# First stage of a two-layer attention and expert kernel: projection placed directly behind the scores, tables cleared from SP's queue, first expert's rows loaded at the stage's end

## The chip, the cores and the metric

The kernel runs as one launch on one core of a Trainium2 chip. The metric is the device time of that core in microseconds (us). The time of the kernel before is 1819.05 us, the median of three runs (1818.01 to 1819.5).

## The reference, cut to what matters

Eight sequences of 100 rows of 512 values pass through two layers. Each layer is an attention over a context and then a mixture of 8 experts, of which each row uses the best two:

```python
x = x + xattn0(layernorm(x), ctx)     # 16 heads of 32, causal: of 722 context rows only the first 100 count
x = x + ffn0(layernorm(x), ...)       # norm again, logits over 8 experts, top 2, gelu(x W1 + b1) W2 + b2, weighted; adds x again
x = x + xattn1(layernorm(x), ctx)     # 16 heads of 64, own rows and 722 context rows as keys
x = x + ffn1(layernorm(x), ...)       # top 2 of 8, silu(gate) * up, down, norm
```

Inside `xattn0`: `q = x q_w + q_b`, `k = ctx k_w + k_b`, `v = ctx v_w + v_b`, `softmax(q k^T / sqrt(32)) v`, then `o_w`, `o_b`. All is float32.

## The kernel before, in words

`build` (L2073) runs seven stages one after the other, and `end_stage` (L100) closes each: GpSimd clears the semaphores, and a barrier of all engines follows. In `front`, the stage that is changed, a barrier also ends its block of five engine programs (L318). The stages are `front` (attention of layer 0, and the routing of each row to its experts), `experts` layer 0, `combine` 0, `project`, `attend`, `experts` layer 1, `combine` 1.

`front` works through the eight sequences, one cycle `b` for each. Every engine has its own program, written out by hand, and runs it strictly in order; semaphores join them. Queries and keys are projected for two sequences at a time (a pair `g` has blocks "q" and "k"), in halves of 16 products into banks 6 and 7. `block_at(b)` (L313) says which block cycle b makes: "k" of pair b//2+1 in even cycles, "q" in odd ones, none in cycles 6 and 7.

The programs in cycle b, before the change:

- TensorE (L575 to L607): `scores(b)` into banks 0 to 3; `values(b)` into bank 4, once `scaled(b-1)` on VectorE has read it (`yn`); `route_logits(b-2)` into bank 7; `output(b-1)` into bank 5; `route_rank(b-2)` into bank 7; the projection `project_pair` (L452); `turn_x(b+3)` into bank 5, after `add_output(b-1)` has read it (`os_`); `turn_probabilities(b)` in four groups q = 0 to 3 into banks 6 and 7, of which q = 1 waits until `route_slot(b-2)` has read bank 7 (`rkc`); `route_turn(b-1)`; `attended(b)`. In cycle 0 a product of the value bias with the output weights (L583) stands behind `values`, and writes `ob`, on which `turn_x(3)` waits (`obs`).
- VectorE (L731 to L756): `scaled`, `highest`, `route_best`, in cycle 0 `vb_wide`, the low part of `o_w` and `ob` (L738 to L742), `add_output`, `route_slot`, `normalise_rows(b+3)`, `projected` (reads banks 6 and 7, adds the bias), `context_low`, `input_stats(b+5)`, `route_rows(b-1)`. After cycle 7 follow `route_best`, `route_slot` and `r.passes`, which lays out the table of expert passes.
- ScalarE (L832 to L845): `attended_high`, `exponents`, `values`, in cycle 0 `weights_high` of `o_w`, `context_high` in even cycles, `turned_x`, `turned`, `route_turned`.
- GpSimd (L412 to L433): `route_root(b-1)`, `root_in(b+5)`, `add_bias(b+1)`; in cycles 0 to 3 twelve transfers each (eleven in the last) that write zeros of 512 KB over the tables `slot_rows` and `slot_outs` in device memory; from cycle 5 on the scatters that put normalised rows into their slots, two for each sequence, after `zeroed`.
- SP (L333 to L368) issues loads: inputs, weights, the context of each pair, and ahead for the next stage three chunks of expert weights.

`experts` layer 0 makes passes of 256 rows. Before its loop SP loads b1, gamma and beta (L917 to L919) and the first rows `xs` (L930, L943); TensorE turns the rows (L984), VectorE (L1052) and ScalarE (L1115) apply gamma and beta once all three constants are in (`c_in` 48, L1037 and L1099), the rows are split into high and low parts (L1123, L1058), and the first product (L1005) starts.

Of the kernel before, what the change touches and what calls it, by code (L numbers as in the profile page):

```python
# [37 lines left out]
CAP = 256  # L38
# [196 lines left out]
def front(k, ahead0):  # L235
# [4 lines left out]
    ZERO_CYCLES = 4  # L240
    with ExitStack() as c:
# [65 lines left out]
        e_hi = k.sem("e0_hi_ahead")  # L307
# [10 lines left out]
        with nc.Block() as block:  # L318
            @block.sync
            def _(sp):  # L320
                def x(b):
                    sp.dma_start(k.x[:, b, :], a["x"][b]).then_inc(x_in[b], 16)
# [29 lines left out]
                for b in range(5, B):  # L352
                    x(b)
                for g in range(2, PAIRS):
                    sp.wait_ge(pjs, first_half(g - 2, "k") + 2)
                    sp.wait_ge(cld, g - 1)
                    context(g)
                for q in range(ahead0.LOADED):
                    if q == 0:
                        sp.wait_ge(wld, 1)  # L360
                    elif q == 1:
                        sp.wait_ge(wld, 2)
                        sp.wait_ge(obm, 1)
                    else:
                        sp.wait_ge(pj, first_half(PAIRS - 1, "k") + 2)
                    sp.dma_start(ahead0.raw[q][:], a[ahead0.names[q][0]][ahead0.names[q][1]]).then_inc(raw_in[q], 16)
                for q in range(ahead0.LOADED):
                    sp.wait_ge(raw_in[q], 16)  # L368

            @block.gpsimd  # L370
            def _(pool):
# [37 lines left out]
                pool.wait_ge(zmade, 1)  # L409
                pool.wait_ge(obs, 1)  # L410
                per = -(-len(ZERO_ROWS) // ZERO_CYCLES)
                for b in range(B):  # L412
                    if b >= 1:
                        route_root(b - 1)
                    if b + 5 < B:
                        root_in(b + 5)
                    if b == 0:
                        add_bias(0)
                    if b + 1 < B:
                        add_bias(b + 1)  # L420
                    if b < ZERO_CYCLES:
                        for dst, n in ZERO_ROWS[per * b:per * (b + 1)]:
                            pool.dma_start(dst[CAP * n:CAP * (n + 1)].rearrange("(p s) d -> p (s d)", p=128),
                                           zero[:]).then_inc(zeroed, 16)
                    if b == 5:
                        pool.wait_ge(zeroed, 16 * len(ZERO_ROWS))
                    if b >= 5:
                        scatter(2 * (b - 5))
                        scatter(2 * (b - 5) + 1)
# [6 lines left out]
            def _(pe):  # L436
# [138 lines left out]
                for b in range(B):  # L575
                    scores(b)
                    values(b)
# [8 lines left out]
                    if b >= 2:  # L586
                        route_logits(b - 2)
# [4 lines left out]
                    if block_at(b):  # L592
                        if b >= 1:
                            pe.wait_ge(ts, 4 * b)
                        else:
                            pe.wait_ge(pjs, 4)
                        project_pair(*block_at(b), ranked=b - 1)
# [18 lines left out]
            def _(dve):  # L616
# [114 lines left out]
                for b in range(B):  # L731
                    if b >= 1:
                        scaled(b - 1)
                    highest(b)
                    if b >= 2:
                        route_best(b - 2)
                    if b == 0:
                        dve.wait_ge(c_in, 32)  # L738
                        nc.vector.tensor_copy(vb_wide[:], bc(vb[:], T)).then_inc(vbw, 1)
                        weights_low(2, wo, "o")  # L740
                        dve.wait_ge(obm, 1)
                        nc.vector.tensor_tensor(ob[:], ob[:], ps[0:T, 5, :], ALU.add).then_inc(obs, 1)  # L742
                    if b >= 1:
                        add_output(b - 1)
                    if b >= 2:
                        route_slot(b - 2)
                    if b + 3 < B:
                        normalise_rows(b + 3)
                    if block_at(b):
                        projected(*block_at(b))  # L750
                    if b % 2 == 0 and b // 2 + 1 < PAIRS:
                        context_low(b // 2 + 1)
                    if b + 5 < B:
                        input_stats(b + 5)
                    if b >= 1:
                        route_rows(b - 1)  # L756
# [12 lines left out]
            def _(act):  # L769
# [62 lines left out]
                for b in range(B):  # L832
                    if b >= 1:
                        attended_high(b - 1)
                    exponents(b)
# [3 lines left out]
                    if b % 2 == 0 and b // 2 + 1 < PAIRS:  # L839
                        context_high(b // 2 + 1)  # L840
# [11 lines left out]
def experts(k, layer, first, s1=None):  # L852
# [18 lines left out]
    with ExitStack() as c:  # L871
# [6 lines left out]
        xs = k.sb(c, L + "xs", [128, 2, D])  # L878
# [34 lines left out]
        with nc.Block() as block:  # L913
            @block.sync
            def _(sp):
                if not gated:
                    sp.dma_start(b1[:], a["b1"]).then_inc(c_in, 16)  # L917
                    sp.dma_start(gam[:], a["gam0"]).then_inc(c_in, 16)
                    sp.dma_start(bet[:], a["bet0"]).then_inc(c_in, 16)  # L919
# [23 lines left out]
                rows(0)  # L943
# [622 lines left out]
class FirstWeights:  # L1566
# [4 lines left out]
    def __init__(self, k, ctx, layer, parts=None):  # L1571
# [5 lines left out]
        self.hi, self.lo = parts  # L1577

# [561 lines left out]
```

## Time and profile before

| | us |
|---|---|
| median of three runs | 1819.05 |
| the profiled execution's own time | 1819.06 |
| its span, first to last instruction | 1817.3 |
| TensorE matmul busy | 1644.4 (90%) |
| VectorE busy | 1080.6 (59%) |
| ScalarE busy | 764.2 (42%) |
| GpSimd busy | 156.2 (9%) |
| mean granted TensorE clock | 0.946 of full speed |

The profile is of one execution. PE is TensorE's matmuls, PEld its weight loads, DVE VectorE, ACT ScalarE, POOL GpSimd, SP the engine that only issues transfers; a q behind a name means that engine's queue. In a timeline a row has the start, the duration, the engine, the line, the operation, output <- input by the program's names, the shapes and the count; in square brackets stands how long the engine was idle before, and who released it. The granted clock is 1.00 at 2.4 GHz and 0.50 at 1.2 GHz. The stage `front` takes the first 228 us of the span, `experts` layer 0 follows.

### The profile page before, as it was taken

How to read it: one execution, taken by the hardware profiler on the slowest of the kernel's cores; microseconds unless marked ns; L12 is line 12 of the kernel's file. 1: busy time of each engine (PE TensorE's matmuls, PEld its weight loads, DVE VectorE, ACT ScalarE, POOL GpSimd, SP SyncE). 2: the span in 40 equal slices, each digit the busy share in tenths (PEclk: the TensorE clock that was granted, in tenths of full speed). 3: DMA queues.
4: the chain of work that ended last, by engine and by line, in shares of the span. 5: the costliest groups of instructions: out<-in, count | busy, mean ns of one | idle time of the engine just before them, and what ended most of it. 6: DMA issues, size and time to landing. Idle time of an engine off the chain costs nothing. (4 is left out here: it accounts for less than half of the span.)

```text
span 1817.3 us, 31629 instructions
## 1 busy us (share of the span) xinstructions
PE 1644.4 (90%) x11976; PEld 1392.7 (77%) x11976; DVE 1080.6 (59%) x1968; ACT 764.2 (42%) x1348; POOL 156.2 (9%) x208
## 2 busy tenths in 40 slices
PE   6888479999999779979999999999999759999984
PEld 5776369999999469768787877878787559999981
DVE  3666656666777652236565655656565557667666
ACT  2333245555555332235354443535353324454440
POOL 1442200000000300100000000000000000000004
PEclk9998689999999889989999999999999769999996
DMA  5871155555555434240111101110202045556534
GB/s 161 333 291 37 37 210 208 208 208 206 204 204 202 135 123 167 82 133 18 47 44 31 52 23 48 27 57 17 60 24 85 10 150 208 209 184 229 208 127 117
DMA packets 86571, 232.81 MB, mean 128 GB/s; under 512 B 33326, under 2 KB 39854, under 8 KB 71374
## 3 DMA queue, kind: packets, MB, share of 16 engines
q1 hardware_dynamic: 68446, 175.52, 28.4%
q0 software_dynamic: 18032, 55.99, 8.7%
q8 instruction: 66, 1.08, 0.2%
q14 instruction: 27, 0.22, 0.0%
HBM read 180.41 MB, written 51.05 MB: 127 GB/s over the span
## 5 line engine op out<-in xcount | busy, mean ns | idle before, releaser
L1727 PE MATMUL banks<-a_ch,a_wm 128*128 128x362 f32 (+1 forms) x1024 | 285.8, 340 | 10.4 <-DVE a_cl L1888 10.4
L1042 DVE TENSOR_TENSOR e_lo<-e_raw,e_hi 128x2048 fp32r<-128x2048 f32 x98 | 224.4, 2290 | 94.8 <-ACT e_hi L1106 94.8
L1005 PE MATMUL banks<-e_xh,e_hi 128*128 128x256 f32 x768 | 217.5, 283 | 4.2 <-DVE e_xl L1058 4.2
L1005 PE MATMUL banks<-e_xh,e_lo 128*128 128x256 f32 x768 | 217.9, 284 | 0.0
L1005 PE MATMUL banks<-e_xl,e_hi 128*128 128x256 f32 x768 | 217.9, 284 | 0.0
L1106 ACT CAST e_hi<-e_raw 128x2048 fp32r<-128x2048 f32 x98 | 186.7, 1905 | 29.4 <-PE banks L1022 29.4
L1727 PEld LDWEIGHTS banks<-a_ch,a_wm 128*128 128x128 f32 x1024 | 186.1, 190 | 12.2 <-DVE a_cl L1888 11.8
L1901 DVE TENSOR_REDUCE a_nmax<-banks 100x1 f32<-100x822 f32 x128 | 123.6, 1007 | 76.1 <-PE banks L1761 75.3
L1727 PE MATMUL banks<-a_cl,a_wm 128*128 128x362 f32 (+1 forms) x512 | 168.8, 330 | 0.0
L1005 PEld LDWEIGHTS banks<-e_xh,e_hi 128*128 128x128 f32 x768 | 147.3, 192 | 10.4 <-issue 4.6
L1022 PE MATMUL banks<-e_hi,e_hh 128*128 128x512 f32 x384 | 152.6, 397 | 0.0
L1005 PEld LDWEIGHTS banks<-e_xl,e_hi 128*128 128x128 f32 x768 | 147.3, 192 | 5.3
L1022 PE MATMUL banks<-e_lo,e_hh 128*128 128x512 f32 x384 | 150.9, 393 | 0.0
L1022 PE MATMUL banks<-e_hi,e_hl 128*128 128x512 f32 x384 | 149.6, 390 | 0.0
L1005 PEld LDWEIGHTS banks<-e_xh,e_lo 128*128 128x128 f32 x768 | 147.3, 192 | 0.0
L2011 ACT ACTIVATE a_P<-banks,a_nmax 100x822 f32<-100x822 f32 x128 | 120.7, 955 | 11.1 <-DVE a_nmax L1901 10.9
L1772 PEld LDWEIGHTS banks<-ident,a_P 100*128 100x128 f32 (+2 forms) x896 | 82.2, 137 | 34.1 <-issue 31.8
L1140 ACT ACTIVATE e_hf<-banks,e_b 128x256 f32<-128x256 f32 x128 | 59.7, 473 | 112.8 <-PE banks L1005 112.7
L1761 PE MATMUL banks<-a_kT,a_q 64*100 64x512 f32 (+1 forms) x512 | 105.3, 530 | 0.0
L1772 PE MATMUL banks<-ident,a_P 100*128 100x100 f32 (+2 forms) x896 | 101.8, 254 | 3.0 <-ACT a_PT L2019 3.0
L1005 PE MATMUL banks<-e_xh,a_wm 128*128 128x256 f32 x512 | 96.2, 287 | 8.8 <-DVE e_hf L1071 5.5
L1727 PEld LDWEIGHTS banks<-a_cl,a_wm 128*128 128x128 f32 x512 | 98.0, 192 | 0.0
(280 smaller groups left out, 3019.9 us busy)
## 6 DMA issues: line engine op xcount, KB each, us to landing
e_raw<-wout SPq DMA_DIRECT2D x50, 1024.0 KB, 7.8
e_raw<-w SPq DMA_DIRECT2D x34, 1024.0 KB, 6.1
e_raw<-wgate SPq DMA_DIRECT2D x17, 1024.0 KB, 5.0
e_raw<-wup SPq DMA_DIRECT2D x17, 1024.0 KB, 5.1
slot_rows<-a_zero POOLq DMA_DIRECT2D x33, 512.0 KB, 9.2
a_craw<-ctxT SPq DMA_DIRECT2D x32, 361.0 KB
e_xs<-slot_rows SPq DMA_DIRECT2D x18, 512.0 KB
slot_outs<-e_y POOLq DMA_DIRECT2D x16, 512.0 KB, 3.2
```

What stands on the lines that cost most here:

```text
L1005: mm = nc.tensor.matmul(ps[:, bank, 0:CAP], w[:, cc, cut], x[:, cc, :], start=t == 0, stop=t == len(terms) - 1)
L1022: mm = nc.tensor.matmul(ps[:, 4 + s, :], h[q % 4][:, cut], w[:, q % 4, :], start=q == 0 and t == 0, stop=q == NB - 1 and t == 2)
L1042: nc.vector.tensor_tensor(lo[g % 2][i], raw[q % RAW][:], hi[g % 2][i].bitcast(F32), ALU.subtract)\
L1106: nc.scalar.copy(hi[g % 2][i], raw[q % RAW][:]).then_inc(hi_done, 1)
L1140: nc.scalar.activation(hf[kb % 4][:], ps[:, kb % 4, 0:CAP], ACT.Gelu, bias=b1[:, bass.ds(e * NB + kb, 1)]).then_inc(f_done, 1)
L1727: mm = nc.tensor.matmul(ps[:, 6 + half, 0:wide], w[:, cc, cut], x[:, cc, start:start + wide], start=cc == 0 and t == 0, stop=cc == DC - 1 ...
L1761: mm = nc.tensor.matmul(ps[0:T, 2 * two + f, 0:wide], q[s][r, :], kT[s][r, first:first + wide], start=True, stop=True)
L1772: mm = nc.tensor.transpose(ps[0:size, 4 + n // 5, T * (n % 5):T * (n % 5) + T], P[(2 * m + two) % 4][:, first:first + size], k.ident[0:T, ...
L1901: nc.vector.tensor_reduce(nmax[:, h:h + 1], two_banks(2 * two)[0:T, 0:KEYS], AX, ALU.max, negate=True)\
L2011: nc.scalar.activation(P[h % 4][:], two_banks(2 * two)[0:T, 0:KEYS], ACT.Exp, bias=nmax[:, h:h + 1], accum_out=sums[:, h:h + 1]).then_inc( ...
```

## The change

Three edits of `front`, with their counterpart in `experts`. First, on TensorE the projection of cycle b stands directly behind `scores(b)`, before `values(b)`; `route_logits`, which writes a bank that the projection has filled, waits until VectorE has read it. On VectorE `projected`, `context_low`, `normalise_rows` and `input_stats` move up, behind `highest`; in cycle 0 `normalise_rows(3)` stays behind `ob`. On ScalarE `context_high` moves ahead of `exponents`. Second, the 47 zero transfers are issued by SP, 23 behind the context of pair 2 and 24 behind that of pair 3, and not by GpSimd. Third, at the end of `front` SP waits for all scatters and loads the first expert's rows there; in `experts` that load goes, and gamma, beta and b1 are issued after it, in this order.

```diff
@@ front, SP
+                sp.wait_ge(zmade, 1)
                 for g in range(2, PAIRS):
                     sp.wait_ge(pjs, first_half(g - 2, "k") + 2)
                     sp.wait_ge(cld, g - 1)
                     context(g)
+                    for dst, n in ZERO_ROWS[(g - 2) * len(ZERO_ROWS) // 2:(g - 1) * len(ZERO_ROWS) // 2]:
+                        sp.dma_start(dst[CAP * n:CAP * (n + 1)].rearrange("(p s) d -> p (s d)", p=128),
+                                     zero[:]).then_inc(zeroed, 16)
...
+                sp.wait_ge(scattered, 32 * B)
+                sp.dma_start(ahead0.xs[:], k.rows[0:CAP, :].rearrange("(s p) d -> p s d", p=128)).then_inc(rows_in, 16)
                 for q in range(ahead0.LOADED):
                     sp.wait_ge(raw_in[q], 16)
+                sp.wait_ge(rows_in, 16)
@@ front, GpSimd
                 pool.memset(zero[:], 0.0).then_inc(zmade, 1)
-                pool.wait_ge(zmade, 1)
                 pool.wait_ge(obs, 1)
...
-                    if b < ZERO_CYCLES:
-                        for dst, n in ZERO_ROWS[per * b:per * (b + 1)]:
-                            pool.dma_start(dst[CAP * n:CAP * (n + 1)].rearrange("(p s) d -> p (s d)", p=128),
-                                           zero[:]).then_inc(zeroed, 16)
@@ front, TensorE
                     scores(b)
+                    if block_at(b):
+                        if b >= 1:
+                            pe.wait_ge(ts, 4 * b)
+                        else:
+                            pe.wait_ge(pjs, 4)
+                        project_pair(*block_at(b), ranked=b - 2)
                     values(b)
...
                     if b >= 2:
+                        if block_at(b):
+                            pe.wait_ge(pjs, first_half(*block_at(b)) + 2)
                         route_logits(b - 2)
                     if b >= 1:
                         output(b - 1)
                     if b >= 2:
                         route_rank(b - 2)
-                    if block_at(b):
-                        if b >= 1:
-                            pe.wait_ge(ts, 4 * b)
-                        else:
-                            pe.wait_ge(pjs, 4)
-                        project_pair(*block_at(b), ranked=b - 1)
@@ front, VectorE
                     highest(b)
+                    if block_at(b):
+                        projected(*block_at(b))
+                    if b % 2 == 0 and b // 2 + 1 < PAIRS:
+                        context_low(b // 2 + 1)
+                    if b + 3 < B and b >= 1:
+                        normalise_rows(b + 3)
+                    if b + 5 < B:
+                        input_stats(b + 5)
                     if b >= 2:
                         route_best(b - 2)
...
                     if b >= 2:
                         route_slot(b - 2)
-                    if b + 3 < B:
-                        normalise_rows(b + 3)
-                    if block_at(b):
-                        projected(*block_at(b))
-                    if b % 2 == 0 and b // 2 + 1 < PAIRS:
-                        context_low(b // 2 + 1)
-                    if b + 5 < B:
-                        input_stats(b + 5)
+                    if b == 0:
+                        normalise_rows(3)
                     if b >= 1:
                         route_rows(b - 1)
@@ front, ScalarE
                         attended_high(b - 1)
+                    if b % 2 == 0 and b // 2 + 1 < PAIRS:
+                        context_high(b // 2 + 1)
                     exponents(b)
                     values(b)
                     if b == 0:
                         weights_high(wo, "o")
-                    if b % 2 == 0 and b // 2 + 1 < PAIRS:
-                        context_high(b // 2 + 1)
@@ experts
-        xs = k.sb(c, L + "xs", [128, 2, D])
+        xs = k.sb(c, L + "xs", [128, 2, D]) if first.xs is None else first.xs
...
-                if not gated:
-                    sp.dma_start(b1[:], a["b1"]).then_inc(c_in, 16)
-                    sp.dma_start(gam[:], a["gam0"]).then_inc(c_in, 16)
-                    sp.dma_start(bet[:], a["bet0"]).then_inc(c_in, 16)
...
-                rows(0)
+                if first.xs is None:
+                    rows(0)
+                else:
+                    sp.sem_inc(x_in, 16)
+                if not gated:
+                    sp.dma_start(gam[:], a["gam0"]).then_inc(c_in, 16)
+                    sp.dma_start(bet[:], a["bet0"]).then_inc(c_in, 16)
+                    sp.dma_start(b1[:], a["b1"]).then_inc(c_in, 16)
```

## Rows read from the trace of the kernel before

**Rows 1.** Stretches: length, busy time by engine (PE, PEld, DVE, ACT, POOL), clock, DMA.

```profile
53.38:72.96 19.58, 17.09 (x184) 14.22 (x180) 11.26 (x20) 7.54 (x24) 11.28 (x18) 1.00 0.99 377
93.79:114.50 20.71, 18.15 (x197) 15.29 (x193) 13.97 (x33) 7.54 (x24) 13.88 (x25) 1.00 0.97 365
```

**Rows 2.** Timeline of PE, cycle 3, from its scores to those of cycle 4.

```profile
97.32 0.47 PE L441 MATMUL banks<-e_hi,a_ctxhi 128*100 128x512 f32 x1 [1.67 <-DVE a_y L669]
103.65 0.26 PE L560 MATMUL banks<-r_sel,r_upper 100*100 100x8 f32 x2
103.94 5.66 PE L466 MATMUL banks<-a_xT,e_raw 128*128 128x200 f32 x32
110.27 0.89 PE L517 MATMUL banks<-ident,a_P 100*100 100x100 f32 x8 [0.32 <-DVE a_qT L641]
112.99 0.89 PE L531 MATMUL banks<-a_PT,a_v 100*32 100x100 f32 x32 [0.24 <-ACT a_PT L804]
114.50 0.97 PE L483 MATMUL banks<-a_mask_r,a_ident_r 100*100 100x400 f32 x4
```

**Rows 3.** Timeline of DVE: add_output, route_slot in cycle 3; route_rows in cycles 3 and 6.

```profile
103.85 0.69 DVE L678 TENSOR_TENSOR x_res<-x_res,banks 100x512 f32<-100x512 f32 x1 [0.44 <-PE banks L441]
105.97 0.15 DVE L193 TENSOR_TENSOR r_taken<-r_taken,banks 100x8 f32<-100x8 f32 x1
110.13 0.60 DVE L692 TENSOR_SCALAR r_rows<-x_res,r_mv,r_rs 100x512 f32<-100x512 f32 x1
168.86 1.43 DVE L692 TENSOR_SCALAR r_rows<-x_res,r_mv,r_rs 100x512 f32<-100x512 f32 x1
```

**Rows 4.** Timeline of PE, cycles 6 and 7, around the granted clock's falls.

```profile
168.43 2.43 PE L517 MATMUL banks<-ident,a_P 100*100 100x100 f32 x12 [1.80 <-DVE r_taken L193]
170.65 0.87 PE L544 MATMUL banks<-ident,r_rows 100*128 100x100 f32 x4
189.79 0.86 PE L517 MATMUL banks<-ident,a_P 100*100 100x100 f32 x8 [1.80 <-DVE r_taken L193]
```

**Rows 5.** Stretches in cycles 6 and 7, columns as in rows 1.

```profile
168.43:176.40 7.97, 6.90 (x80) 5.28 (x81) 2.49 (x6) 1.97 (x4) 5.56 (x6) 0.50 0.34 92
176.40:182.00 5.60, 5.36 (x42) 3.93 (x42) 4.80 (x4) 0.52 (x1) 0.00 (x0) 0.50 0.05 18
182.00:187.20 5.20, 5.20 (x30) 3.87 (x29) 2.98 (x13) 4.21 (x17) 0.00 (x0) 1.00 0.00 0
```

**Rows 6.** Timeline of cycle 0: the bias product, o_w's low part, ob, x turned.

```profile
38.90 3.68 PE L583 MATMUL banks<-e_raw,a_vb_wide 128*100 128x512 f32 x8 [1.22 <-DVE a_vb_wide L739]
42.72 2.04 ACT L786 CAST e_hi<-e_raw 128x2048 fp32r<-128x2048 f32 x1
44.79 2.29 DVE L652 TENSOR_TENSOR e_lo<-e_raw,e_hi 128x2048 fp32r<-128x2048 f32 x1 [5.94 <-ACT e_hi L786]
48.28 0.54 PE L448 MATMUL banks<-ident,a_xn 100*128 100x100 f32 x4 [0.29 <-DVE a_xn L629]
```

**Rows 7.** Closing drain of GpSimd's queue in front, project and attend: count, ns, start.

```profile
L318 POOLq DRAIN  x1: 5213/5213/5213, 222.4 to 222.4; - x1
L1367 POOLq DRAIN  x1: 2016/2016/2016, 779.7 to 779.7; - x1
L1651 POOLq DRAIN  x1: 1359/1359/1359, 1467.7 to 1467.7; - x1
```

**Rows 8.** Timeline across the stage boundary, SP and PE.

```profile
228.78 0.33 SPq L917 DMA_DIRECT2D e_b<-b  x1
230.32 0.38 SPq L930 DMA_DIRECT2D e_xs<-slot_rows  x1
233.93 1.97 PE L984 MATMUL banks<-ident,e_xs 128*128 128x128 f32 x8 [17.54 <-DMA e_xs<-slot_rows]
235.99 1.51 ACT L1115 ACTIVATE e_xf<-banks,e_bet,e_gam 128x128 f32<-128x128 f32 x4 [24.50 <-PE banks L984]
240.10 0.57 PE L1005 MATMUL banks<-e_xh,e_hi 128*128 128x256 f32 x1 [4.21 <-DVE e_xl L1058]
```

More of the change, by code:

```diff
@@ L239, in front @@
     ZERO_ROWS = [(k.rows, r) for r in range(E * SPAN // CAP + 1)] + [(k.outs, r) for r in range(PASSES)]
-    ZERO_CYCLES = 4
     with ExitStack() as c:
@@ L306, in front @@
         raw_in = [k.sem(f"e0_raw_in{q}") for q in range(ahead0.LOADED)]
-        e_hi = k.sem("e0_hi_ahead")
+        e_hi, rows_in = k.sem("e0_hi_ahead"), k.sem("e0_rows_in")
         def first_half(g, which):
@@ L408, in _ @@
                 pool.memset(zero[:], 0.0).then_inc(zmade, 1)
-                pool.wait_ge(zmade, 1)
                 pool.wait_ge(obs, 1)
-                per = -(-len(ZERO_ROWS) // ZERO_CYCLES)
                 for b in range(B):
@@ L1577, in __init__ @@
         self.hi, self.lo = parts
+        self.xs = k.sb(ctx, f"e{layer}_xs", [128, 2, D]) if layer == 0 else None
 def attend(k, s1, ahead1):
```

## The prediction

> **What bounds the kernel now.** I read the stage's own stretches first, then TensorE's timeline inside one cycle, then the clock, then the stage boundary. In cycles 1 and 3 TensorE is busy 17.1 of 19.6 us and 18.2 of 20.7 us at full clock, while VectorE, ScalarE and GpSimd have a third or more of the cycle free [rows 1]. So a cycle of `front` is as long as TensorE's program plus its waits. The largest wait of cycle 3 is 1.67 us: `values` stands behind the scores until VectorE has made y from the sequence before. Small ones are 0.32 us for the projection's read and 0.24 us for the last copy of turned probabilities [rows 2]. In cycles 6 and 7, which project nothing, the q=1 group of turned probabilities waits 1.80 us for `route_slot` [rows 4]. Close behind each of these two waits the granted clock falls to 0.50 (1.2 GHz): 168.43 to 176.40 has 0.50, 182.00 to 187.20 has 1.00 again [rows 5]. From 222.4 us on nothing computes: GpSimd's queue drains for 5.2 us, the barrier follows, and the first rows are turned at 233.93 and multiplied at 240.10 [rows 7, 8]. The later stages are not touched, and I take what `front` and the boundary gain or lose to reach the end one to one.
>
> **The stage's end and the next one's start.** The length of GpSimd's closing drain follows the number of transfers that GpSimd has issued in its block. `attend` has 16 scatters and 1.36 us, `project` 24 stores (4, 4 and 16, by the listing of transfers and the code) and 2.02 us, `front` 47 zero transfers and 16 scatters, 63, and 5.21 us [rows 7]. That is 0.085, 0.084 and 0.083 us each. With 16 left `front`'s drain should last 1.36 us and end near 223.8, not 227.6.
>
> The Trainium skill ("DMA: Bandwidth & Descriptors", section "Issuing engines are not separate DMA queues") says that transfers from all issuing engines end on the same 16 DMA engines, and that spreading them saves only issue time. GpSimd's issue time is hidden here, so by that rule this edit is worth nothing; the drain rows say otherwise.
>
> What is late next is the new wait for the first rows. POOL's drain begins at 222.4 [rows 7], so its wait for the scatters passed near 222.2. SP now issues the rows there, and from issue to use they took 3.6 us (230.32 to 233.93) [rows 8]. They land at 225.85; the barrier follows 1.75 us earlier than before. Nothing is queued behind SP's wait but the block's end, and that is what the other engines wait for.
>
> In `experts` PE then starts when its table load is done. SP's first issue after the barrier was at 228.78, and I allow 1.15 us more for PE's register work: 229.95, so 228.2 in the new run. The turn takes 1.97 and ends at 230.2. The next bound is the constants: b1, now the third of three issues of 0.33 to 0.43 us, leaves SP near 227.9 and lands 2 to 3.6 us later; the lower end is an estimate, the upper the 512 KB rows' own 3.6 [rows 8]. I take 2.9 and get 230.8. From xf's start to the first product it was 4.1 us (235.99 to 240.10) [rows 8]: 234.9, so -5.2. Bounds: -3.5 (the clearing semaphore or the drain does not shrink) to -6.0 (constants earlier).
>
> **Zero transfers on SP.** The 47 issues at some 0.35 us are issued from about 38 us on by an engine that only waits. They move 24.6 MB; at the 377 GB/s that cycle 1 shows with the DMA engines 0.99 busy [rows 1], some 65 us, done near 105. The zeros' consumer, the first scatter, comes at 149. Context 2 is issued ahead of the zeros, context 3 between the halves, some 30 us of backlog before a use at about 115; the expert chunks behind them are used at 190. All is covered: 0. Without that cover context 3 would stop a projection. GpSimd's own operations between the zeros are off TensorE's path: 0.
>
> **Cycles 1 to 5.** New order in cycle 3: scores 1.86 (93.79 to 97.32 less the 1.67 idle), projection 5.5, values to rank 6.33 (97.32 to 103.65) [rows 2]. y is ready 3.5 us into the cycle, hidden by the projection: 1.67 and 0.32 go. But the projection had also covered VectorE's work behind `output`. `add_output` ends 0.9 us after rank begins, and r_taken, which frees bank 7 for q=1, at 2.5 us (103.65 to 105.97 + 0.15) [rows 2, 3]; q=1 starts at +2.6. In between TensorE has only `turn_x` and q=0, 0.95 us. This is cycle 6's wait [rows 4], now in cycles 2 to 5 too. `route_rows` follows `route_slot` at once and meets GpSimd's `add_bias`: 1.43 us in place of 0.60, as in cycle 6 [rows 3]. From q=1 to `attended` I get 2.45, then 1.5 (112.99 to 114.50) [rows 2]: rank to next scores 6.55. Sum 13.7 + 6.55 = 20.25 against 20.7: -0.4 a cycle, -1.6 for four (bounds 0 and -1.2 a cycle, the waits that go in full). Cycle 1 has no routing yet: 1.67 + 0.32 go, 1.0 comes for `turn_x`, 0.2 for `route_turn`: -0.8.
>
> **Cycle 0.** The projection runs from 34.35 to 39.85, `values` to 42.7. VectorE reaches `vb_wide` only behind `projected`, `context_low` and `input_stats`, near 42.8, so the bias product of 3.7 us runs to 46.5. ScalarE copies v only now, the cast of o_w starts 0.65 later, its low part too, and `turn_x(3)`, at 48.28 before [rows 6], starts at 48.95. The projection's read is no longer waited for, so the scores of cycle 1 start +0.2. But TensorE idles from 46.5 to 48.95: 2.4 us ahead of a run of small transposes, longer than the 1.80 us ahead of the two falls in the trace [rows 4]. I expect the clock to fall there. Cost by the rows at 0.50: transposes 0.87 for four against 0.51 [rows 4], five groups, part behind copies, +1.3; `attended` +1.4 (twice); scores +1.4; of the projection behind them 2.8 us at half speed before the clock returns, +1.4, as the clock came back after some 2 us of dense products in cycle 7 [rows 5]. Together +5.5, bounds 4.1 (back as the projection starts) and 8 (it stays low for most of it).
>
> **Cycle 5** has no `turn_x`: its tail is cycle 6's, rank, q=0, 1.8 us of nothing. So I put a fall there: three transposed groups +0.7, `attended` +1.4, scores +1.4, values +1.0, less the wait for y that slow scores swallow, -1.4: +3.1 (0 to 5). Cycles 2 to 4 have two gaps of 0.8 and 0.7 us with `turn_x` and q=0 between them; I take no fall. Cycles 6 and 7 keep theirs.
>
> **Sum.** -5.2 - 1.6 - 0.8 + 0.2 + 5.5 + 3.1 = +1.2. Against the profiled execution's own 1819.06, 0.01 from the median of the runs, this gives 1820.3 us.
>
> **Rivals.**
> - Only cycle 0 falls. 1820.3 - 3.1 = 1817.2. For it: the moment at which such a gap comes may decide. Against: cycles 6 and 7 are alike in this and both fell.
> - No new fall: the reordering costs nothing, and the boundary gives its 5.2. 1819.06 - 7.4 = 1811.7. For it: the full clock held through waits of 1.67 us in cycles 1 to 5. Against: 2.4 us is longer than any of these, and transposes follow. The Trainium skill ("TensorE: Matmul & The Clock Gate", section "Why this matters for your kernels") names a longer idle gap than any here as what drops the clock, and would have this case; the falls behind 1.80 us speak against it.
> - The slower side: the waits moved behind `output` drop the clock in cycles 2 to 4 as well. There a fall costs the 5.5 of cycle 0, since a projection follows. One such fall gives 1825.8, two 1831.3; it decides from the first. For it: gaps of 1.5 us in 2.6. Against: `turn_x` and q=0 split them.
>
> That the boundary edit does nothing (drain unchanged) would add 1.7 to each.
>
> **Chances.** Faster or slower by 0.2%, 3.6 us, is what a measurement of this kernel can tell: below 1815.4, above 1822.7. Forecast 0.34 (own range 1817 to 1824; 0.02 faster, 0.27 same, 0.05 slower); one fall 0.20 (0.06 faster, 0.14 same); none 0.22, all faster; falls in cycles 2 to 4 0.24, all slower. Together 0.30, 0.41, 0.29. The range reaches from the no-fall case, 1811.2, to one further fall and 1 us of the bounds, 1827.0.
>
> **What would show it.** Right: POOL's drain at L318 near 1.4 us; the first product of `experts` 12.7 us after the last scatter has landed (222.2 here) and not 17.9; no idle time ahead of `values`; L517 released by r_taken with over 1 us idle in cycles 2 to 5; L448 of cycle 0 behind 2.4 us of idle time, and granted clock 0.50 soon after it. Wrong: clock 1.00 throughout cycles 0 to 5 (then the time is near 1812), a drain still of 5 us, or a PE wait on a transfer between 40 and 110 us.

## The result, and the profile after

The changed kernel takes 1823.68 us (median of 12 runs, 1820.42 to 1827.72) against 1819.35 for the kernel before in the same comparison; the ratio is 1.0023, 95% interval [1.0014, 1.0032]. It is 4.2 us slower, where 1.2 had been forecast. The kernel before measured 1814 to 1821 us from one comparison to the next, so everything below goes by ratios to the kernel before of the same comparison; a difference of ratios is turned into us by multiplying it by 1819. A fall is a moment at which TensorE's granted clock goes from 1.00 (2.4 GHz) to 0.50 (1.2 GHz).

The cycles 0 to 7 of `front` in the kernel after, each from its scores to the next (columns as in [rows 1]: length, busy time of PE, PEld, DVE, ACT, POOL, granted clock, DMA share, GB/s):

```profile
32.09:55.17 23.08, 20.22 (x172) 15.24 (x172) 12.44 (x19) 8.70 (x23) 5.26 (x6) 0.86 0.73 282
55.17:75.30 20.13, 18.89 (x184) 15.45 (x181) 12.35 (x20) 7.63 (x24) 2.46 (x3) 0.91 1.03 392
75.30:95.29 19.99, 18.14 (x196) 15.34 (x192) 15.91 (x37) 8.28 (x25) 2.49 (x3) 1.00 1.03 412
95.29:116.89 21.60, 19.81 (x196) 16.62 (x192) 13.88 (x33) 7.62 (x24) 1.96 (x2) 0.92 0.61 234
116.89:138.71 21.82, 20.21 (x196) 17.04 (x192) 14.43 (x34) 8.38 (x25) 1.95 (x2) 0.89 0.14 50
138.71:163.98 25.27, 23.18 (x192) 19.09 (x188) 13.57 (x32) 7.43 (x23) 5.82 (x6) 0.77 0.07 19
163.98:185.25 21.27, 16.34 (x158) 11.74 (x157) 12.42 (x30) 7.22 (x23) 5.86 (x7) 0.82 0.15 41
185.25:208.60 23.35, 19.11 (x159) 13.72 (x157) 11.62 (x30) 9.02 (x24) 5.04 (x6) 0.65 0.17 50
```

The same cycles of before lasted 20.90, 19.58, 20.83, 20.71, 20.73, 20.79, 20.38 and 20.47 us, the first six at clock 1.00 [rows 1 has cycles 1 and 3]. The differences are +2.18, +0.55, -0.84, +0.89, +1.09, +4.48, +0.89 and +2.88: together +12.1. Only cycle 2, the one whose clock stayed at 1.00, is shorter. The stretches of cycles 0 to 7 and of what follows them, up to 219 us, in which the clock stood at its lower level, 1.2 GHz, in the same execution:

```profile
48.80:58.40 9.60, 9.01 (x118) 7.22 (x116) 3.06 (x2) 2.46 (x5) 2.26 (x2) 0.50 1.02 406
113.80:116.89 3.09, 3.09 (x67) 2.56 (x65) 0.22 (x1) 0.49 (x1) 0.00 (x0) 0.50 0.00 0
134.40:144.00 9.60, 9.60 (x114) 8.14 (x115) 5.71 (x8) 1.70 (x4) 0.29 (x1) 0.50 0.01 3
158.20:171.40 13.20, 11.54 (x117) 8.31 (x116) 7.29 (x8) 2.29 (x5) 4.91 (x5) 0.50 0.23 64
185.60:195.20 9.60, 8.37 (x48) 5.41 (x48) 5.72 (x5) 2.58 (x11) 0.00 (x0) 0.50 0.10 31
202.60:219.00 16.40, 12.26 (x96) 9.29 (x96) 8.93 (x18) 3.85 (x6) 3.43 (x4) 0.50 0.18 52
```

Four falls are new, in cycles 0, 3, 4 and 5; the last two rows stand for the two that the kernel before has in cycles 6 and 7. TensorE's timeline in the kernel after shows what lies ahead of them (L466 is the projection, L441 the values' product, L448 x turned, L517 probabilities turned):

```profile
48.33 0.55 PE L448 MATMUL banks<-ident,a_xn 100*128 100x100 f32 x4 [2.23 <-DVE a_xn L631]
97.09 5.68 PE L466 MATMUL banks<-a_xT,e_raw 128*128 128x200 f32 x32
102.46 0.53 PE L441 MATMUL banks<-e_hi,a_ctxhi 128*100 128x512 f32 x1
109.79 0.56 PE L448 MATMUL banks<-ident,a_xn 100*128 100x100 f32 x4 [0.50 <-DVE x_res L680]
111.47 0.86 PE L517 MATMUL banks<-ident,a_P 100*100 100x100 f32 x8 [0.77 <-DVE r_taken L193]
133.14 0.86 PE L517 MATMUL banks<-ident,a_P 100*100 100x100 f32 x8 [0.77 <-DVE r_taken L193]
141.90 6.84 PE L466 MATMUL banks<-a_xT,e_raw 128*128 128x200 f32 x32
157.45 2.07 PE L517 MATMUL banks<-ident,a_P 100*100 100x100 f32 x12 [1.80 <-DVE r_taken L193]
```

The 1.67 us ahead of L441 [rows 2] are gone: 102.46 has no wait. In its place stand 0.50 and 0.77 us behind the rank in cycles 2 to 4, 1.80 in cycle 5, and 2.23 in cycle 0. Cycle 2 has the same two waits as cycles 3 and 4, and no fall. The projection that begins at 141.90 runs at half speed at first and takes 6.84 instead of 5.68.

At the boundary, SP's and PE's timelines of the kernel after, to be held against [rows 8]:

```profile
234.20 0.38 SPq L371 DMA_DIRECT2D e_xs<-slot_rows  x1
```

```profile
240.61 1.94 PE L991 MATMUL banks<-ident,e_xs 128*128 128x128 f32 x8 [12.22 <-DVEq L1035]
246.75 0.58 PE L1012 MATMUL banks<-e_xh,e_hi 128*128 128x256 f32 x1 [4.21 <-DVE e_xl L1065]
```

And GpSimd's closing drain in `front`, against [rows 7]:

```profile
L317 POOLq DRAIN  x1: 1375/1375/1375, 234.4 to 234.4; - x1
```

The rows' load is issued at 234.20, as the last scatter has landed, and the first product of `experts` starts 12.55 us later; before it was 17.9. The scatters landed 12.0 us later than before (222.2 and 234.2: cycle 0 began 0.4 earlier, the cycles took 12.1 and the tail 0.3 more), so the first product starts 6.65 us late (240.10 to 246.75), and the span ends 5.0 us late (1817.3 to 1822.3).

### The profile page after: what moved, and what is told of

Read it like the earlier page. It is cut to its first block and busy times, and to the rows that moved or that the text cites. A ratio compares the mean times of both kernels' runs of the same rounds, so it can differ in the third digit from the quotient of the medians.

```text
span 1822.3 us, 31638 instructions
## 1 busy us (share of the span) xinstructions
PE 1655.6 (91%) x11976; PEld 1401.2 (77%) x11976; DVE 1083.4 (59%) x1968; ACT 764.3 (42%) x1348; POOL 130.2 (7%) x161
```

## The experiments

**First: the change taken apart.** The theory at this point, with its rival in each expectation: the new order lengthens the stage through the clock alone, and the boundary gives its 5 us whatever the order is. `e1_order` has the new order and nothing else, `e2_edges` the other two edits without it, `e3_zeros` and `e4_rows` one of these each (zeros on SP, and rows loaded at the stage's end).

```diff
 e1_order: before, with
+                    scores(b)
+                    ... project_pair(*block_at(b), ranked=b - 2)
+                    values(b)
 and the moves on VectorE and ScalarE; zeros from GpSimd, rows loaded in experts
 e2_edges: after, with these moves undone
 e3_zeros: e2_edges, rows loaded in experts as before
 e4_rows:  e2_edges, zeros from GpSimd as before
```

> The kernel before with the reordering alone (TensorE, VectorE and ScalarE programs of the changed kernel; zero transfers stay on GpSimd, first rows stay in the next stage). Clock theory (the waits moved behind the output product let TensorE's clock fall in cycles 0 and 3 to 5): the stage up to the landing of the last scatter takes 12 us longer than the 222.2 us of before, at the boundary nothing is gained, and the time is 7 to 11 us above the kernel before, near 1829; granted clock 0.50 in part of cycle 0 and of two or more of cycles 2 to 5. Rival (the zero transfers on SP's queue slow the stage, the order is harmless or good): no more than 1819, and clock 1.00 through cycles 1 to 5.

> The changed kernel without the reordering: zero transfers on SP, first expert's rows loaded at the stage's end. Clock theory: cycles 0 to 7 as in the kernel before (20.9, 19.6, 20.8, 20.7, 20.7, 20.8 us), the last scatter lands near 222.2, the first product of the experts comes 12.6 us behind it and not 17.9, and the time is 5.3 us below before, near 1814. Rival (SP's backlog costs the stage): the cycles between 38 and 101 us are longer, and the gain is under 3 us or gone.

> The kernel before with only the zero transfers moved from GpSimd to SP. If the drain at the stage's end goes with the number of transfers that GpSimd issued: POOL's drain 1.37 us in place of 5.21, time 3.8 us below before, near 1815.5. If the drain is the fixed price of the scatters: drain 5.2 us, time within 1 us of before.

> The kernel before with only the first expert's rows loaded at the stage's end (zero transfers stay on GpSimd), constants behind. The rows land in 3.6 us, under the drain of 5.2 us, which still sets the barrier; behind the barrier the rows need not be waited for: 3.5 to 4.0 us below before, near 1815.5. The two edges are then not additive: together 5.3, apart 3.8 each, since the rows' 3.6 us become what is late when the drain shrinks. Rival (they are independent): rows alone gives 1.5 us, so that the sum is 5.3.

| | us, median (runs) | ratio to before, 95% | in us |
|---|---|---|---|
| order alone | 1829.57 (6) | 1.0052 [1.0034, 1.0071] | +9.5 |
| zeros and rows | 1814.96 (8) | 0.9967 [0.9955, 0.9979] | -6.0 |
| zeros alone | 1816.56 (12) | 0.9980 [0.9968, 0.9992] | -3.6 |
| rows alone | 1817.24 (12) | 0.9978 [0.9967, 0.9989] | -4.0 |

The parts add up: +9.5 - 6.0 = +3.5 against +4.2 for the whole change. The order is all of the loss. The profile of `e1_order` has its new falls in the same cycles as the changed kernel, 0, 3, 4 and 5; its stage ends 16.3 us late and not 12, but that execution, 1835.16 us, was one of the two slowest of six. The zeros' and the rows' edits give 3.6 and 4.0 us, as expected; the rival's 1.5 us for the rows lies outside the interval (-6.0 to -2.0). Together they give 6.0 rather than 7.6, which the intervals do not tell apart, but the profiles do: from the scatters' landing to the first product of `experts` it took 17.9 us before, 14.1 with the rows alone (223.72 to 237.84), 14.0 with the zeros alone (about 223.3 to 237.32) and 12.55 with both, 5.3 less and not 7.7. Each edit shortens one of two things that pass beside each other, the drain and the rows' load. In the profile of `e2_edges` the boundary came out as expected, but not the cycles: cycle 0 began at 36.42, 4 us late, and cycle 2 has a short stretch at the lower clock and took 22.41 us instead of 20.8; the other cycles up to 5 are as before. GpSimd's drain, in `e3_zeros` and then in `e4_rows`:

```profile
L317 POOLq DRAIN  x1: 1375/1375/1375, 223.5 to 223.5; - x1
```

```profile
L318 POOLq DRAIN  x1: 5213/5213/5213, 223.9 to 223.9; - x1
```

**Second: is it the clock, or the waits themselves?** `f1_filled` keeps the order of the changed kernel and puts products that nobody needs (the filler) into the waits of cycles 0 and 2 to 5.

```diff
 after, with
+ def keep_busy(b, at):
+     n = FILL.get((b, at), 0)      # cycle 0, before turn_x: 8;  cycles 2 to 4, before turn_x: 2
+     if n:                         # cycles 2 to 4, before q=1: 3;  cycle 5, before q=1: 7
+         pe.wait_ge(e, 4 * b + 4)
+     for _ in range(n):
+         nc.tensor.matmul(ps[0:T, 3, 0:4 * T], ident_r[:], mask..., start=True, stop=True)
```

> The changed kernel with products of the identity and the mask (128x100 by 100x400, into a bank already read, result unused) put on TensorE in its own waiting gaps: 8 ahead of the rows' turn in cycle 0, 2 ahead of that turn and 3 ahead of the second probability turn in cycles 2 to 4, 7 ahead of the second probability turn in cycle 5. They add work that the output does not need and take none away. Clock theory (the order costs time only through TensorE's clock, which falls behind the gaps of cycles 0, 3, 4 and 5): no granted clock of 0.50 between 30 and 165 us; the order is then worth the shorter cycles alone, so 1815.0 (the kernel without the order) less 2.2 = 1812.8, 11 under the changed kernel's 1824. Rival, the new waits themselves are on the path and the clock is only their companion: the filler changes nothing or costs its own time, 1822 to 1828, even where the clock stays at 1.00. Second rival, filler longer than the gap: each block of 3 delays its cycle by up to 0.5 us, 1814 to 1816.

1802.95 us against 1814.34, ratio 0.9932 [0.9916, 0.9949]: 12.4 us under the kernel before and 16.5 under the changed one (0.9932 / 1.0023), more than the 11 expected. More work, and the kernel is faster: the clock it was. The mean granted clock of all its six executions is 0.949 to 0.955, that of the changed kernel's twelve 0.936 to 0.941. A row of its filler in cycle 3, where the 0.77 us of idle time stood, and cycles 0 to 6 of `f1_filled`:

```profile
108.57 0.77 PE L515 MATMUL banks<-a_mask_r,a_ident_r 100*100 100x400 f32 x3
```

```profile
34.27:55.05 20.78, 19.01 (x181) 14.38 (x181) 12.44 (x19) 8.41 (x23) 5.26 (x6) 1.00 0.70 266
55.05:73.48 18.43, 17.19 (x184) 14.14 (x180) 12.29 (x20) 7.52 (x24) 2.48 (x3) 1.00 1.02 391
73.48:93.41 19.93, 19.18 (x201) 15.90 (x197) 15.93 (x37) 8.28 (x25) 2.50 (x3) 1.00 1.03 412
93.41:113.47 20.06, 19.30 (x202) 15.91 (x198) 13.88 (x33) 7.62 (x24) 1.96 (x2) 1.00 0.86 335
113.47:133.51 20.04, 19.27 (x201) 15.91 (x197) 14.44 (x34) 8.37 (x25) 1.96 (x2) 1.00 0.16 54
133.51:153.60 20.09, 19.09 (x200) 15.96 (x196) 13.50 (x32) 7.22 (x23) 3.76 (x4) 1.00 0.02 4
153.60:171.64 18.04, 14.43 (x160) 11.20 (x157) 12.42 (x30) 7.22 (x23) 7.27 (x8) 0.86 0.22 63
```

With the clock at 1.00 the new order is shorter than the old one in every cycle: by 0.12, 1.15, 0.90, 0.65, 0.69 and 0.70 us, 4.2 in all. Against the changed kernel cycles 0 and 1 give back 4.0 (23.08 + 20.13 less 20.78 + 18.43), cycles 3 to 5 give back 8.5, and cycle 6 3.2. No fall is left in cycles 0 to 5.

`f2_cycle0_old` takes away one of the four gaps by leaving cycle 0 in its old order on TensorE and VectorE.

```diff
 after, with
-                    if block_at(b):
+                    if b >= 1 and block_at(b):
                         ... project_pair directly behind scores
+                    if b == 0:
+                        pe.wait_ge(pjs, 4)
+                        project_pair(*block_at(b))      # behind values, as before
```

> The changed kernel with cycle 0 in the old order and cycles 1 to 7 in the new one. Clock theory: the fall at 48.7 us goes and nothing else does, cycle 0 takes 20.9 instead of 23.1 and cycle 1, which began at the low clock, about 1 less: 3 to 5 us under the changed kernel, 1819 to 1821. Rival, the falls are tied to each other (a fall that goes only moves the next one forward): 1823 to 1826, with a fall in cycle 1 or 2 in place of that in cycle 0.

1815.43 us, ratio 1.0001 [0.9986, 1.0016]: 4.0 under the changed kernel (1.0023 and 1.0001), as the clock theory said. But the rival has a part in it too. Cycles 0 to 2 of `f2_cycle0_old`:

```profile
33.90:54.80 20.90, 17.82 (x173) 13.10 (x173) 12.35 (x19) 8.40 (x23) 4.23 (x6) 1.00 0.70 267
54.80:73.23 18.43, 17.19 (x184) 14.14 (x180) 12.30 (x20) 7.52 (x24) 3.29 (x4) 1.00 1.02 387
73.23:94.52 21.29, 19.45 (x197) 16.52 (x193) 15.94 (x37) 8.28 (x25) 2.51 (x3) 0.93 1.04 414
```

Cycles 0 and 1 are 3.9 us shorter, and now cycle 2 has a fall that it had not, and is 1.3 longer. Cycles 2 to 4 have the same gaps; which of them falls differs: here it is 2 and 4 (91.6 and 132.5 us), in the changed kernel 3 and 4. What decides between them stays open. Of its twelve executions eleven took 1812 to 1820 us at mean clocks of 0.940 to 0.944, and one 1805.07 at 0.951.

`f3_split` looks for an order that has the gain without the gaps: half of the projection behind the scores, half behind the rank.

```diff
 e2_edges, with, for b >= 1,
                     scores(b)
+                    project_pair(*block_at(b), ranked=b - 2, halves=(1,))
                     values(b)
 ...
                     route_rank(b - 2)
-                    project_pair(*block_at(b), ranked=b - 1)
+                    project_pair(*block_at(b), halves=(0,))
 and VectorE reads the halves where they are made; its and ScalarE's other moves as in after
```

> The boundary as in the changed kernel; in cycles 1 to 5 only the half of the projection that goes to bank 7 stands directly behind the scores, the other half stays where it was, behind the rank; cycle 0 in the old order. Clock theory: half the projection's columns (about 1.7 us) are enough to cover the wait for the reciprocals behind the scores, the other half still covers the waits behind the rank, so no new fall in cycles 0 to 5, and each of the cycles 1 to 5 is 1.0 to 1.8 us shorter than the old one: 1815.0 - 5 x 1.4 = 1808, 1806 to 1810. Rival, the gaps of 0.5 to 0.8 us in front of the turns come back with half the cover and the clock falls as in the changed kernel: 1815 to 1820. Rival, VectorE's order bounds the cycle and not TensorE's: 1815, cycles of 20.7 as before.

1801.68 us, ratio 0.9926 [0.9912, 0.9940], 13.5 us under the kernel before and 7.5 under `e2_edges`. Cycles 0 and 3 to 5 of `f3_split`, and under them two rows of cycle 4 in its PE timeline:

```profile
33.01:55.23 22.22, 19.12 (x172) 14.27 (x172) 12.35 (x19) 9.17 (x24) 5.01 (x6) 0.94 0.72 276
...
93.55:112.62 19.07, 18.08 (x196) 15.29 (x192) 12.97 (x33) 7.54 (x24) 1.97 (x2) 1.00 0.85 325
112.62:131.75 19.13, 18.14 (x197) 15.23 (x193) 13.73 (x34) 8.29 (x25) 1.95 (x2) 1.00 0.17 57
131.75:150.85 19.10, 17.77 (x192) 14.87 (x188) 12.55 (x32) 7.05 (x23) 5.08 (x5) 1.00 0.07 18
```

```profile
114.42 2.97 PE L466 MATMUL banks<-a_ctx,e_raw 128*128 128x200 f32 x16
...
127.52 0.89 PE L517 MATMUL banks<-ident,a_P 100*100 100x100 f32 x8 [0.42 <-DVE a_kT L647]
```

Cycles 3 to 5 are 1.6 to 1.7 us shorter than in the old order, cycle 1 1.4 and cycle 2 0.7: half the projection, 2.97 us, is enough to hide the wait for y, and the other half still covers `add_output` and `route_slot`. The wait of 1.67 is gone from these cycles and 0.42 is what stands ahead of the first turned probabilities. "No new fall in cycles 0 to 5" was a miss, though: the clock falls in cycle 0 (52.4 us), which is 1.3 us longer than before. TensorE's program there is the one of before, and its waits behind the projection, 0.58 us at most, are the same in the kernel before, where the clock held.

`f4_filled67` asks whether the two falls that both kernels have, in cycles 6 and 7, can be filled as well.

```diff
 e2_edges, with
+ FILL = {(6, before q=1): 7, (7, before q=1): 7}
```

> The order of before, the boundary as changed, and 7 filler products ahead of the second probability turn in cycles 6 and 7, where TensorE stood 1.80 us in both kernels and its clock fell in both. Clock theory: both falls (168.4 and 189.8 us of the kernel before) go, each worth 2.1 to 5.5 us: 1815.0 - 2 x 4 = 1807, 1804 to 1811. Rival, these gaps only happen to lie ahead of the falls, and the thin work behind them (turns of 128x128, little else) brings the clock down in any case: 1815 to 1816, with falls within 5 us of the same places.

1806.92 us, ratio 0.9958 [0.9944, 0.9972]: 7.6 us under the kernel before, of which `e2_edges` has 6.0, so the filler is worth 1.6 and not 8, and with these intervals (some 2.5 us to each side) the 1.6 is not told apart from nothing. Yet in the profiled execution it does all that was asked. Cycles 6 and 7:

```profile
154.97:171.35 16.38, 13.85 (x168) 10.56 (x164) 12.43 (x30) 7.12 (x23) 3.81 (x4) 1.00 0.05 13
171.35:187.56 16.21, 13.71 (x167) 10.54 (x163) 11.63 (x30) 8.20 (x24) 5.43 (x7) 1.00 0.21 60
```

They last 16.38 and 16.21 us, against 20.38 and 20.47 before. That execution took 1801.69 us and was the fastest of the five; the other four lie between 1806.47 and 1808.86. Its mean granted clock was 0.956, that of the other four 0.950 to 0.952. So they had more time at the lower clock; that it is one of these two falls come back is argued, not shown, since no stretches are known of them.

**Third: the last two together, both kernels once more, and the drain.** `g1_split_filled67` joins `f3_split` and `f4_filled67`; `g2_before_again` and `g3_after_again` are second profiles of the two kernels; `g4_half_zeros` tests the drain.

```diff
 g4_half_zeros: before, with
-                            pool.dma_start(dst[CAP * n:CAP * (n + 1)]..., zero[:])
+                            for part in range(2):
+                                first = CAP * n + part * CAP // 2
+                                pool.dma_start(dst[first:first + CAP // 2]..., zero[:, 0:CAP * D // 256])
```

> Projection split as in the kernel with half of it behind the scores, and in addition 7 filler products ahead of the second probability turn in cycles 6 and 7 (they add work that the output does not need). Clock theory: cycles 6 and 7 take 16.2 to 16.4 us as in the kernel with this filler alone, against 20.4 in both older ones; the split alone measured 0.9926 of the kernel before, the filler alone 2.4 us beyond the boundary's gain in the median and some 8 us in its profiled run. So 2.4 to 8 us under the split: 0.988 to 0.991 of the kernel before. Rival, the low stretch is only put off to the next gap (the stage's tail, where TensorE stands 3.2 to 3.8 us): within 1 us of the split, 0.9920 to 0.9930.

> The kernel before once more, unchanged, for a second profile of it. If its low stretches are set by its own gaps: cycles 1 to 5 without a low stretch, falls in 6 and 7 at the same two gaps, start of each within 2 us of the first profile's, relative to the cycle. If they are set by something outside of the kernel: low stretches in other cycles. Ratio to itself 0.999 to 1.001 either way.

> The changed kernel once more, unchanged, for a second profile. Clock theory: a fall in cycle 0 behind the 2.2 us gap and one behind the 1.80 us gap of cycle 5 again; in cycles 2 to 4, whose gaps of 0.5 and 0.8 us are marginal, one to three falls that need not be in the same cycles as in the first profile. Ratio 1.0014 to 1.0035. If the falls of cycles 3 and 4 were an accident of one execution: none or one there, and a ratio under 1.001.

> The kernel before with each of GpSimd's 47 transfers of zeros cut in two of half the size: 94 transfers, the same bytes. If the drain at the block's end costs by the number of transfers that GpSimd has issued (16 transfers 1.375 us, 63 transfers 5.213 us in the kernels so far: 0.0817 us each): 110 transfers drain in 9.05 us, and the time is 3.8 us longer, ratio 1.002 (GpSimd's own issue time doubles too, but beside slack). Rival, it costs by the bytes or by what is still under way: 5.2 us as before, ratio 1.000.

`g1_split_filled67`: 1810.08 against 1820.70, ratio 0.9929 [0.9913, 0.9945], no different from the split alone and the rival's number, not the 0.988 to 0.991 of the theory; its runs spread from 1804.68 (mean clock 0.953) to 1816.26 (0.947). The profiled one is the slowest. Apart from the stage's end it has falls in cycle 0 (55.2 us, low up to 62.1), at the start of cycle 6 (157.7) and at the start of cycle 7 (178.1), so the split order does not keep the clock up in every execution either. In its PE timeline, ahead of the last of these falls, the filler (L515) stands in cycle 6, the wait is down to 0.43 us, and the clock falls all the same, behind the last products of `attended`, which stop three times for 0.36 us with "issue" as the cause, that is, waiting for nothing that the profile shows:

```profile
169.42 1.50 PE L515 MATMUL banks<-a_mask_r,a_ident_r 100*100 100x400 f32 x7
171.35 0.90 PE L528 MATMUL banks<-ident,a_P 100*100 100x100 f32 x8 [0.43 <-DVE r_taken L193]
...
176.75 0.39 PE L547 MATMUL banks<-a_PT,a_ones 100*32 100x100 f32 x5 [0.37 <-issue]
177.50 0.38 PE L547 MATMUL banks<-a_PT,a_ones 100*32 100x100 f32 x4 [0.36 <-issue]
```

```profile
177.90:188.30 10.40, 8.80 (x52) 6.11 (x52) 5.72 (x5) 3.14 (x13) 0.22 (x1) 0.51 0.11 33
```

So filling one gap is no remedy by itself. The same three stops stand ahead of the fall at 157.7 in this profile and of that at 185.3 in the changed kernel. Whether they bring the clock down or only go with it stays open.

`g3_after_again`: ratio 1.0021 [1.0011, 1.0031]. Its cycles 0 to 5:

```profile
32.57:55.98 23.41, 20.55 (x172) 15.59 (x172) 12.44 (x19) 8.72 (x23) 5.25 (x6) 0.85 0.73 282
55.98:77.38 21.40, 20.16 (x185) 16.75 (x181) 12.39 (x20) 7.65 (x24) 2.48 (x3) 0.85 1.03 393
77.38:97.33 19.95, 18.10 (x196) 15.33 (x193) 15.94 (x37) 8.29 (x25) 2.51 (x3) 1.00 1.02 413
97.33:119.31 21.98, 20.69 (x197) 17.58 (x193) 13.87 (x33) 7.73 (x24) 1.95 (x2) 0.87 0.52 202
119.31:141.57 22.26, 20.59 (x196) 17.18 (x192) 14.43 (x34) 8.51 (x25) 1.96 (x2) 0.88 0.13 49
141.57:167.09 25.52, 23.21 (x193) 19.27 (x189) 13.56 (x32) 7.35 (x23) 5.78 (x6) 0.77 0.07 20
```

The same cycles fell, 0, 3, 4 and 5, and cycle 2 again did not, as the theory allowed. The falls of cycles 3 and 4 were no accident of one execution.

`g2_before_again`: ratio 1.0001 [0.9992, 1.0010]. Cycles 1, 3, 4 and 5 take what they took, 19.57, 20.71, 20.73 and 20.76, and cycles 6 and 7 fall again (174.4, 2.3 us later in its cycle, and 194.9 us); but, against the expectation, cycle 2 has a short low stretch behind the 1.66 us ahead of `values`:

```profile
75.15:97.53 22.38, 19.84 (x196) 16.25 (x193) 14.79 (x37) 8.39 (x25) 8.50 (x15) 0.92 0.79 321
```

The old order does not always keep the clock up in cycle 2 either. Of the seven profiles with the old order in that cycle, three show this, `e2_edges`, `g2_before_again` and `g4_half_zeros`; in these three cycle 0 began at 33.45 us or later, in the four others at 32.66 or earlier.

`g4_half_zeros`: ratio 1.0022 [1.0012, 1.0032], +4.0 us, where 3.8 had been worked out, and the drain:

```profile
L318 POOLq DRAIN  x1: 9052/9052/9052, 226.7 to 226.7; - x1
```

Same bytes, twice the zero transfers, and 9.05 us, as the rule by their number gave. Their bytes don't count, and neither do the packets into which the DMA queue cuts them: from 33 to 140 us the queue of GpSimd's transfers has 6768 packets before and 7520 here, a ninth more, for a drain that is 74% longer.

## Why the prediction was right where it was, and wrong where it was

The time, 4.2 us above the kernel before, lies inside the stated range and 3 us from the forecast, but the mechanism was not the forecast one: it was that of the rival on the slower side, whose price was too high. By the prediction's own line for "slower", 3.6 us, the result is on the side to which it gave 0.29, and not in "same", which had 0.41. That the number is so near is luck in part: terms that came out 9 us worse are partly offset by others that came out better. Term by term:

- **The boundary, -5.2: right.** Drain 1.375 us (1.36 forecast), first product 12.55 us behind the last scatter (12.7 forecast), which is 5.3 less than before; the two edits together measured -6.0 [-8.2, -3.8]. Inside the term two small misses cancel: the turn of the rows began 6.4 us after the scatters had landed and not 6.0, and the constants, to which 2.9 us had been given as the later bound, were not late at all (b1's issue ends at 240.75, and xf starts at 242.64, as the turn ends). With the drain unchanged (`e4_rows`) the first product came 1.6 us later, where 1.7 had been put. What set the drain's length, the number of GpSimd's transfers, is shown by `g4_half_zeros`. The Trainium skill ("DMA: Bandwidth & Descriptors", section "Issuing engines are not separate DMA queues") would have moved zeros save issue time only. The DMA engines are indeed as full as before while the zeros move (1.03 against 0.99 in cycle 1), so this case agrees on that; but the issuing engine's drain is a cost on top, 3.84 us in these rows.
- **Zeros on SP, 0: right.** No PE wait between 40 and 110 us is put down to a transfer, and `e3_zeros` and `e2_edges` show no cost beside the boundary's gain. The issues did not take 0.35 us each, though, but 1.2 (23 of them 28.05 us from 38.78 on, in the kernel after), so they held SP up to 99.1 us; nothing that is needed early stood behind them.
- **Cycles 0 to 5 at full clock, -2.2 in all: right in sign, half the size.** `f1_filled`, with its filler in the waits, has -4.2, cycle 2 of the changed kernel -0.84 where -0.4 was taken. The waits were forecast as 0.8, 0.7 and 1.8 us and came out as 0.50, 0.77 and 1.80. The sign named for them, L517 behind r_taken with over 1 us idle in cycles 2 to 5, contradicts these 0.7 us and came true in cycle 5 alone.
- **The fall in cycle 0, +5.5: right.** It came behind 2.23 us of idle time (2.4 forecast) and cost 4.0 us in the first profile, just under the lower bound of 4.1, and, by the same sum with `g3_after_again`, 5.6 in the second. The difference is when the clock came back: at 58.9 us, half a microsecond into the projection, in the first (so that of the 1.4 put for the projection 0.3 came), and at 62.4 in the second, where the projection took 7.08 us, 1.4 more than at full clock.
- **"Cycles 2 to 4 ...; I take no fall": this is the step that failed.** Two of the three fell, in both profiles of the changed kernel. Cycles 3 to 5 cost 8.5 us more than at full clock, not the 3.1 of one fall in cycle 5. Cycles 3 and 4 have no 1.8 us in one piece: ahead of their falls stand gaps of 0.50 and 0.77 us with 1 us of transposes between them. The argument against this rival, that `turn_x` and q=0 split the gap, is what failed. That the gaps alone decide is not shown: cycle 2 has the same ones and held its clock in both profiles, and in `f3_split` the clock fell in cycle 0 though no wait behind the projection there is over 0.58 us. Shown is that with these waits filled no fall is left in cycles 0 to 5 (`f1_filled`), and that neither profile of the split order has one in cycles 1 to 5.
- **"Cycles 6 and 7 keep theirs": failed too.** They lasted 44.6 us and not 40.9, +3.8: cycle 6 began in the low stretch left by cycle 5 (158.20 to 171.40), and the next one (185.60 to 195.20) lay over the head of cycle 7.
- **The later stages, one to one: off by 1.7 us.** From the first product of `experts` to the end of the span it was 1577.2 us before and 1575.6 after; the twelve profiles of the experiments have 1574.0 to 1577.1, without a visible order.

The cycles therefore lost 12.1 us and not 6.4; with the boundary and the later stages that is +5.0 in the profiled span. The rival on the slower side, falls in cycles 2 to 4 as well, had the mechanism right and the price wrong: it put two further falls at 11 us and the time at 1831.3, and with the 3.1 of cycle 5 that is 14.1 where 8.5 were measured. (A slip without consequence: the range's lower end calls 1811.2 the case of no fall, which the rivals have as 1811.7.) In the first profile cycles 3 to 7 cost 9.2 more than forecast (8.5 - 3.1, and 3.8); cycle 0's fall cost 1.5 less, and the gain at full clock was 2.0 larger: 6.4 + 9.2 - 1.5 - 2.0 = 12.1.

The rule weighed beside the rival of no fall (the Trainium skill, "TensorE: Matmul & The Clock Gate", section "Why this matters for your kernels"), which asks to avoid idle gaps between bursts of matmuls that are longer than any here, does not cover this case. Every gap ahead of the falls of cycles 3 and 4 is under 0.8 us, and they fell.

## What to carry to other kernels

Before moving dense TensorE work forward to cover one wait, look at what is left where it stood: behind small transposes with sub-microsecond waits between them the granted clock fell here in two of three cycles, and what follows then runs at half speed, here for 3 to 14 us each time. Try to split the dense block, so that a part stays at each place; with the same boundary edits the half-and-half order gained 13.5 us where the whole move lost 4.2. And count the transfers that GpSimd issues in a block, not their bytes: the block's end waits about 0.082 us for each.

The best kernels of this study are the split (0.9926), the split with filler (0.9929) and the filled one (0.9932); they are not told apart. The split does it without needless work. It does not rid the kernel of falls: both profiles of the split order have one in cycle 0. Look at more than one profile before you put a fall down to one gap.

## What the runs showed of the hardware that was not expected

- GpSimd's closing drain took 1.375 us after 16 transfers, 5.213 after 63 and 9.052 after 110: 0.082 us for each further transfer, long after their data had landed (the zeros end more than 90 us earlier).
- TensorE's clock fell from 2.4 to 1.2 GHz in cycles whose longest wait was 0.77 us (at 113.6 us in the kernel after). In that profile 0.5 us (48.33 to 48.8, cycle 0) to 6.4 us (178.92 to 185.3, cycle 6) passed between the end of a cycle's longest wait and the fall; in the kernel before the fall of cycle 6 came at 168.4, as the wait of 1.80 us ended.
- The clock does not fall in the same places each time the same program runs: of the two profiles of the kernel before, the second alone has a low stretch in cycle 2.
- Products that nobody needs, put into these waits, made the changed kernel 16.5 us faster.
